# Routing the first expert phase in two halves, with larger DMA pieces and a reordered middle

## The reference

```
x = x + 0.5 * ffn(layernorm(x))
x = x + attn(layernorm(x))
x = x + 0.5 * ffn(layernorm(x))

ffn(x):  logits = x @ gate_w;  e = argmax(logits);  s = sigmoid(max(logits))
         shared = (silu(x @ sg) * (x @ su)) @ sd
         routed = (silu(s*x @ g[e]) * (s*x @ u[e])) @ d[e]
         return shared + routed
```

## Time and profile before

| | before |
|---|---|
| median of three runs | 646.51 us |
| the profiled execution, its own time | 639.84 us |
| its span | 638.1 us |
| TensorE busy | 545.6 us (86%) |
| VectorE busy | 453.0 us (71%) |
| ScalarE busy | 381.3 us (60%) |
| GpSimd busy | 147.9 us (23%) |
| moved by DMA | 40.69 MB, 52655 packets |

### The profile page before, as it was taken

How to read it: one execution, slowest core, us unless ns; L and a number is a source line. 1 busy time by engine, 2 the same in 40 slices (tenths; PEclk the granted TensorE clock), 3 DMA queues, 4 the chain that set the end, 5 groups by cost and what they waited for, 6 DMA issues and landing times.

```text
span 638.1 us, 13759 instructions
## 1 busy us (share of the span) xinstructions
PE 545.6 (86%) x4592; PEld 213.9 (34%) x4593; DVE 453.0 (71%) x832; ACT 381.3 (60%) x814; POOL 147.9 (23%) x236
## 2 busy tenths in 40 slices
PE   2983999935578999999999999999999977899991
PEld 2642344413221222222222222222224434534440
DVE  6561334436479899999999999999996567434442
ACT  2210344414322899999999999999997744134440
POOL 2563144534330000000000000000000034214552
PEclk9997899977655899999999999999999999889997
DMA  9997232221451000100001010000000001112114
GB/s 233 320 334 219 75 88 85 69 79 43 132 168 43 13 2 3 51 2 26 29 2 52 3 50 5 3 2 2 3 2 2 1 19 35 34 33 60 51 38 142
DMA packets 52655, 40.69 MB, mean 64 GB/s; under 512 B 5257, under 2 KB 49950, under 8 KB 52592
## 3 DMA queue, kind: packets, MB, share of 16 engines
q1 hardware_dynamic: 49520, 35.58, 19.2%
q0 software_dynamic: 3072, 4.28, 2.0%
HBM read 26.85 MB, written 14.88 MB: 65 GB/s over the span
## 4 chain that ended last, share of the span: by engine, by line
PE 71%; DVE 13%; DMA 6%; issue 4%; ACT 2%; POOL 2%; SPq 1%; POOLq 0%; ACTq 0%; DVEq 0%
PE bank L1399 22%; PE pair L1376 18%; PE pair L1264 8%; PE bank L1281 5%; DVE rowmax L1031 4%; PE pair L1273 3%; DMA xe<-rows 3%; PE pair L1124 2%; PE bank L1187 2%; POOL rows L514 2%; PE pair L1116 2%; ACT oT L747 1%; PE bank L1252 1%; PE bank L1388 1%; PE bank L1330 1%
## 5 line engine op out<-in xcount | busy, mean ns | idle before, releaser
L1031 DVE TENSOR_REDUCE rowmax<-pair 128x1 f32<-128x1024 f32 x256 | 294.6, 1217 | 15.6 <-PE pair L1376 15.5
L734 ACT ACTIVATE arena<-bank 128x512 f32<-128x512 f32 x500 | 271.1, 597 | 30.7 <-PE bank L1388 23.6
L1376 PE MATMUL pair<-k_stack,q_stack 48*128 48x512 bf16 x512 | 162.7, 403 | 11.0 <-DVE rowmax L1031 10.1
L1399 PE MATMUL bank<-arena 128*32 128x256 f32 x2048 | 161.3, 393 | 3.1 <-ACT oT L747 0.7
L1388 PE MATMUL bank<-q_stack,k_stack 51*128 51x512 bf16 x500 | 152.2, 387 | 0.4 <-ACT arena L734 0.4
L521 POOL DMA_INDIRECT y<-yb,slot_token x64 | 62.9, 982 | 97.9 <-ACT yb L647 94.0
L981 DVE TENSOR_TENSOR arena<-pair,arena 128x256 f32<-128x256 f32 x64 | 27.2, 425 | 78.9 <-ACT arena L642 70.6
L1399 PEld LDWEIGHTS bank<-arena 128*32 128x32 f32 x2048 | 43.4, 108 | 98.5 <-issue 63.5
L1264 PE MATMUL pair<-w_exp,xeT 128*64 x128 | 68.7, 619 | 0.4 <-ACT xeT L637 0.4
L1266 PE MATMUL pair<-w_exp,xeT 128*64 128x512 f32 x128 | 68.7, 619 | 0.0
L1376 PEld LDWEIGHTS pair<-k_stack,q_stack 48*128 48x128 bf16 x512 | 28.4, 95 | 117.8 <-DVE rowmax L1031 83.8
(11 more groups left out here) (187 smaller groups left out, 579.8 us busy)
## 6 DMA issues: line engine op xcount, KB each, us to landing
xe<-rows SPq DMA_DIRECT2D x64, 66.0 KB
w_exp<-in_r_gate SPq DMA_DIRECT2D x4, 1024.0 KB, 10.8
w_exp<-in_r_up SPq DMA_DIRECT2D x4, 1024.0 KB, 10.7
w_exp<-in_r_down SPq DMA_DIRECT2D x8, 512.0 KB, 10.6
rows<-empty_row SPq DMA_DIRECT2D x1, 2112.0 KB, 11.4
rows<-empty_row SPq DMA_DIRECT2D x32, 66.0 KB, 3.5
xnT<-y SPq DMA_DIRECT2D x8, 256.0 KB, 3.4
q_parts<-arena SPq DMA_DIRECT2D x12, 128.0 KB, 2.2
```

The lines of the kernel that those rows point to most:

```text
L734: nc.scalar.activation(prob[c % 2 * GH + head_of(u, c, k)], ring_bank("score", STEPS * u + i), ACT.Exp, scale=SCALE).then_inc(prob_ready, 1)
L1031: nc.vector.tensor_reduce(rowmax[u % 2][:, m:m + 1], pair[j % 2][:, :], AX_X, ALU.max).then_inc(smax_read, 1)
L1376: ins = nc.tensor.matmul(pair[j % 2][:, part * BANK:(part + 1) * BANK], q_stack[r][rows, half, l, t * P:(t + 1) * P], k_stack[r][rows, l, ...
L1399: ins = nc.tensor.matmul(bank[6][32 * h:32 * (h + 1), cols], v_grp[u % 2][:, c, h, :], prob[c % 2 * GH + h][:, cols], start=(c == 0 and w ...
```

## The change

- `TILES_OF` has four parts instead of three: the first phase's tiles 0 to 7 and 8 to 15, the second phase's 0 to 11 and 12 to 15. All uses of the part number follow (2 and 3 for the second phase).
- First phase: rows are normalised in two halves. `choose` is divided into `tops` (the maximum) and the rest. The first half is ranked and placed by its own counts, the second behind them (`ranks_behind(1)`, `more_pages(1)`, three more operations in `place_quad`). The logits of the second half go to another PSUM bank. The shared expert's products stand at other places between these steps, TensorE's `ranks(0)` ahead of `sh_up(0)`, `page_owners` behind `sh_up(5)`.
- Tokens lie otherwise in the tiles: partition p of a batch holds the tokens 8p to 8p+7, so that loads of x and of results and the store of the output move four tiles' rows of a partition in one piece (2 KB instead of 512 B). The token numbers that GpSimd writes into the rows follow.
- Blank rows are stored four at a time (2112 B instead of 528 B). The down matrices are loaded as pairs of rows (1 KB instead of 512 B), one DMA for eight experts instead of two; the expert product is written in the order that fits this.
- SyncE's first four page loads go ahead of the first four blank stores.
- GpSimd clears the attention's stacks behind the first phase's scatters.
- Middle: `store_norm(UNITS - 1)` goes behind the first placed quad instead of the third; in `ffn(1)` the fourth shared product and its Silu go ahead of the last quad's routing.

```diff
-TILES_OF = ((0, TILES), (0, FIRST_TILES), (FIRST_TILES, TILES))
+TILES_OF = ((0, TILES // 2), (TILES // 2, TILES), (0, FIRST_TILES), (FIRST_TILES, TILES))
...
+    def quad_rows(rows, g):
+
+        part = rows[g // 2 * BATCH_TILES * P:(g // 2 + 1) * BATCH_TILES * P, :].rearrange("(p t) h -> p t h", t=BATCH_TILES)
+        return part[:, 4 * (g % 2):4 * (g % 2) + 4, :]
...
+        blank_rows = q_stack[2][:, :, :, :].rearrange("p a l t -> p (a l t)").bitcast(F32)[:, 0:BLANKS * ROW]
...
-        ranks_bank = (bank[3], bank[0], bank[3])
-        ranks_at = [ranks_bank[k][:, 0:EXPERTS * (last - first)] for k, (first, last) in enumerate(TILES_OF)]
-        counts_at = (bank[4][:, 0:EXPERTS], bank[0][:, FIRST_TILES * EXPERTS:(FIRST_TILES + 1) * EXPERTS],
-                     bank[3][:, 4 * EXPERTS:5 * EXPERTS])
+        eid_row_at = (bank[3][0:1, 2 * P:3 * P], bank[3][0:1, 2 * P:3 * P])
+
+
+        ranks_area = (bank[3], bank[2], bank[0], bank[3])
+        logits_bank = (bank[2], bank[7], bank[2], bank[2])
+        ranks_at = [ranks_area[k][:, 0:EXPERTS * (last - first)] for k, (first, last) in enumerate(TILES_OF)]
+        counts_at = [bank[4][:, 0:EXPERTS]] + [ranks_area[k][:, EXPERTS * (last - first):EXPERTS * (last - first + 1)]
+                                              for k, (first, last) in enumerate(TILES_OF) if k]
...
-            sp.dma_start(rows_dram[0].rearrange("(j p) r -> p j r", p=P),
-                         empty_row[:, :].unsqueeze(1).broadcast_to([P, TURNS, ROW])).then_inc(prefilled[0], 16)
+            sp.dma_start(rows_dram[0].rearrange("(p j k) r -> p j (k r)", p=P, k=BLANKS),
+                         blank_rows.unsqueeze(1).broadcast_to([P, SLOTS // P // BLANKS, BLANKS * ROW])).then_inc(prefilled[0], 16)
...
-                for c in range(2):
-                    sp.dma_start(w3[:, e:e + step, 2 * INNER + c * P:2 * INNER + (c + 1) * P],
-                                 r_down[e:e + step, c * P:(c + 1) * P, :].rearrange("e p h -> p e h")).then_inc(experts_loaded, 16)
+
+                sp.dma_start(w3[:, e:e + step, 2 * INNER:],
+                             r_down[e:e + step].rearrange("e (p c) h -> p e (c h)", c=2)).then_inc(experts_loaded, 16)
...
-                    if n == 0:
-                        sp.dma_start(rows_dram[1][bass.ds(j * P, P), :], empty_row[:, :]).then_inc(prefilled[1], 16)
 
                 for r in range(4):
                     load(r, r)
+                if n == 0:
+                    for r in range(4):
+                        clear(r)
                 with sp.Fori(1, TURNS // 4) as k:
                     for r in range(4):
                         load(4 * k + r, r)
+                        if n == 0:
+                            clear(4 * k + r)
...
+            nc.gpsimd.memset(blanks[:, :, 0:P], 0.0)
+            nc.gpsimd.memset(blanks[:, :, P:ROW].bitcast(I32), NOWHERE).then_inc(consts_ready, 1)
             nc.gpsimd.memset(empty_row[:, 0:P], 0.0)
-            nc.gpsimd.memset(empty_row[:, P:ROW].bitcast(I32), NOWHERE).then_inc(consts_ready, 1)
+            nc.gpsimd.memset(empty_row[:, P:ROW].bitcast(I32), NOWHERE)
...
+                    clear_stacks()
...
-            clear_stacks()
...
-                    transposed(0)
+                    transposed(0, 0, 2)
+                    transposed(0, 2, 4)
                     score_exp(0)
+                    score_exp(1)
                 else:
                     for i in range(3):
                         sh_silu(i)
                     transposed(2, QUADS - 1)
-                    score_exp(2)
-                for i in range(3 * n, 2 * QUADS):
+                    sh_silu(3)
+                    score_exp(3)
+                for i in range(4 * n, 2 * QUADS):
...
+            def tops(k):
+
+                tiles = slice(*TILES_OF[k])
+                if k == 2:
+                    dve.wait_ge(pv_done, CHUNKS * (UNITS - 2))
+                dve.wait_ge(logits_ready, k + 1)
+                nc.vector.tensor_reduce(top[:, tiles], by_tile(logits_bank[k])[:, tiles], AX_X, ALU.max).then_inc(top_ready, 1)
...
+            def used_pages():
+
+                nc.vector.tensor_scalar(full_to[:, :], count_i[:, :], float(PAGE), None, ALU.add)
+                nc.vector.tensor_copy(more_i[:, 0:1], spare_to[:, EXPERTS:EXPERTS + 1])
+                after(nc.vector.tensor_tensor(spare_2[:, :], spare_at[:, :], count_i[:, :], ALU.subtract))
+                after(nc.vector.tensor_tensor(spare_2[:, :], spare_2[:, :], base_e[:, :], ALU.subtract))
...
-                if k == 2:
+                if k % 2:
...
-                    normalize(0)
+                    normalize(0, 0, 2)
+                    normalize(0, 2, 4)
+                    tops(0)
                     choose(0)
                     chances(0)
+                    weigh_rows(0)
+                    tops(1)
+                    spare_pages(0)
+                    place_quad(0, 0)
+                    place_quad(0, 1)
                     sh_product(0, 0)
-                    weigh_rows(0)
-                    spare_pages(0)
-                    for g in range(QUADS):
-                        place_quad(0, g)
-                        if g < 3:
-                            sh_product(0, g + 1)
+                    used_pages()
+                    choose(1)
+                    chances(1)
+                    weigh_rows(1)
+                    sh_product(0, 1)
+                    more_pages(1)
+                    place_quad(1, 2)
+                    sh_product(0, 2)
+                    place_quad(1, 3)
+                    sh_product(0, 3)
...
-                    choose(2)
-                    chances(2)
-                    weigh_rows(2)
-                    more_pages()
-                    place_quad(2, last)
                     sh_product(1, 3)
+                    tops(3)
+                    choose(3)
+                    chances(3)
+                    weigh_rows(3)
+                    more_pages(3)
+                    place_quad(3, last)
...
-                    nc.vector.tensor_tensor(h_sb[r % 2], bank[r % 2][:, INNER:2 * INNER], silu_sb[r % 2][:, 0:INNER],
-                                            ALU.mult).then_inc(h_done, 1)
+
+                    by_pair = lambda a: a.rearrange("p (i c) -> p i c", c=2)
+                    nc.vector.tensor_tensor(h_sb[r % 2].rearrange("p (c i) -> p i c", c=2), by_pair(bank[r % 2][:, INNER:2 * INNER]),
+                                            by_pair(silu_sb[r % 2][:, 0:INNER]), ALU.mult).then_inc(h_done, 1)
...
-                choose(1)
-                chances(1)
-                weigh_rows(1)
-                spare_pages(1)
-
-                for g in range(QUADS - 1):
-                    place_quad(1, g)
-                nc.vector.tensor_scalar(full_to[:, :], count_i[:, :], float(PAGE), None, ALU.add)
-                nc.vector.tensor_copy(more_i[:, 0:1], spare_to[:, EXPERTS:EXPERTS + 1])
-                after(nc.vector.tensor_tensor(spare_2[:, :], spare_at[:, :], count_i[:, :], ALU.subtract))
-                after(nc.vector.tensor_tensor(spare_2[:, :], spare_2[:, :], base_e[:, :], ALU.subtract))
+                tops(2)
+                choose(2)
+                chances(2)
+                weigh_rows(2)
+                spare_pages(2)
+
+                place_quad(2, 0)
                 store_norm(UNITS - 1)
+                place_quad(2, 1)
+                place_quad(2, 2)
+                used_pages()
...
-            def ranks_behind():
-
-                pe.wait_ge(slots_ready, 2 * QUADS - 1)
-                for t in range(FIRST_TILES):
-                    hot = onehot[1][:, t * EXPERTS:(t + 1) * EXPERTS].unsqueeze(1).broadcast_to([P, 5, EXPERTS])
-                    nc.tensor.matmul(bank[3][:, 0:5 * EXPERTS].rearrange("p (b e) -> p b e", e=EXPERTS), onesb[:, :], hot,
+            def ranks_behind(k):
+
+                first, last = TILES_OF[k]
+                blocks = last - first + 1
+                if k == 3:
+                    pe.wait_ge(slots_ready, 2 * QUADS - 1)
+                for t in range(first):
+                    hot = onehot[k // 2][:, t * EXPERTS:(t + 1) * EXPERTS].unsqueeze(1).broadcast_to([P, blocks, EXPERTS])
+                    nc.tensor.matmul(ranks_area[k][:, 0:blocks * EXPERTS].rearrange("p (b e) -> p b e", e=EXPERTS), onesb[:, :], hot,
                                      start=(t == 0), stop=False)
...
+                    ranks(0)
                     sh_up(0)
-                    ranks(0)
+                    ranks_behind(1)
                     sh_up(1)
+                    ranks(1)
                     sh_up(2)
                     sh_up(3)
                     sh_down(0)
-                    page_owners()
                     sh_up(4)
                     sh_up(5)
+                    page_owners()
```

(37 more changed lines are left out.)

58 lines of the change are left out of this document (29 added, 29 removed).

## The result

The changed kernel took 638.01 us in the median (637.26 to 638.81, 4 runs) against 646.20 us of the kernel before on the same chip: a ratio of 0.9875, 95% interval 0.985 to 0.9899. Two later sets on other occasions gave 0.9929 (0.9903 to 0.9954; 639.27 us, before 644.13 in 27 runs) and 0.9914 (0.9881 to 0.9947; 640.26 us, before 644.92). By the medians it is 4.7 to 8.2 us faster. The time lies inside the range on record, but the gain is well short of the 13.0 us that the sum promised: the profiled execution took 637.26 us (span 635.5), where the sum gave 626.8.

What follows compares the result with a forecast made beforehand. GpSimd's scatter queue was taken to set the first expert phase, with DMA full beside it. Gains of 5.8 (first phase), 0.3 (before attention), 6.0 (middle) and 0.9 (ends) made 13.0, from 646.51 to 633.5 us; range 627 to 641.

Steps and rivals of the forecast that it cites:

- Routing of the first phase: First expert phase, in two halves: first scatter at 28.4 (5.4 us earlier), ninth at 39.3, sixteenth at 48.3 (4.8 earlier).
- The rival of a late second half: First routing: second half comes four us late, 9.0 us gained in all, 637.5 us; chance 0.16.
- The stream's end, 51.5: First phase: with larger pieces the weight stream ends at about 51.5 instead of 57.3, hidden.
- First phase, 5.8: Routing and page loads of the first phase: second page lands at 59.05 instead of 64.85, 5.8 us gained.
- 58.2 here at most: 0.9 of slack: First phase: the shared expert's tail, 15.7 us after 42.5, ends by 58.2, leaving 0.9 us of slack.
- Middle, 6.0: End of attention to second expert phase: the reorder gains 6.0 us, bounds 3.35 and 7.
- From there to the maximum (536.46) the order is kept: Middle, VectorE from residual to maximum: same order, so the residual's 3.5 us gain carries through, about 3.35 earlier.
- Ends: Results' return and output store in 2 KB pieces: 0.9 us gained; with the 0.3 before attention, bounds 0 and 2.
- Larger pieces in the stream: First-phase weight stream: 367 GB/s for 293 (down weights, 2.9 us) and 257 (blank rows, 3.0 us), hidden.
- no penalty shows: Expert product written with a stride of 128: no penalty expected from 0.425 us; up to some 1.65 us is free.
- the likeliest case's own range: Whole kernel, likeliest case: 633.5 us with its own range 630 to 637.5; chance 0.62.
- a late second half together with a small middle: Whole kernel, both shortfalls at once (first routing late, middle giving only 3.35): would still save 6.5 us.

Runs made afterwards that it cites:

- before, again: Kernel before, unchanged, profiled a second time: 643.98 us in the median, profiled span 643.7.
- pieces: Kernel before with only the larger DMA pieces, their token order and the strided product: 0.9972 of before, 1.8 us.
- middle: Kernel before with only the reordered middle and the fourth shared product's move: 0.998 of before, 1.3 us.
- middle, stop: Kernel before with the reordered middle, GpSimd stopping before the second routing's ninth scatter until the last quad's logits are written: 638.96 us, 0.9901 of before.
- halves: Changed kernel with pieces, token order and middle taken back, leaving the split first routing, page-load order and later stack clearing: 0.9953 of before, 3.0 us.
- after, again: Changed kernel, unchanged, profiled a second time: first page at 58.11 us.
- after, third: Changed kernel, unchanged, profiled a third time: first page at 64.25 us.
- after, stop: Changed kernel, GpSimd stopping before the second routing's ninth scatter until the last quad's logits are written: 633.35 us, 0.9811 of before.
- after, pace 1.8: Changed kernel with the shorter GpSimd memset before each of scatters two to twelve of the second routing: 633.93 us, 0.9807 of before.
- after, pace 2.2: Changed kernel with the longer GpSimd memset before each of scatters two to twelve of the second routing: 635.29 us, seen once.
- after, stop and void wait: Changed kernel with the second-routing stop, plus a first-routing wait for the first shared-expert down-projection that did not pause GpSimd: 632.22 us, 0.9804 of before.
- after, two stops: Changed kernel with the second-routing stop, plus one before the first routing's ninth scatter until the fifth shared-expert piece is written: 630.61 us, 0.9766 of before.

## Why the prediction was right, and where it was wrong

Every profile cut at the same marks (us; "tail" is the end of the last shared-expert addition of the first phase; the third and fourth lengths count from the second phase's first row scatter):

| profile | tail | first page | first scatter to last maximum | to first page | turns | last store to end |
|---|---|---|---|---|---|---|
| before | 54.0 | 63.0 | 16.5 | 39.2 | 68.4 | 10.4 |
| before, again | 63.0 | 64.0 | 18.9 | 40.0 | 71.8 | 10.7 |
| pieces | 63.1 | 64.1 | 18.9 | 40.0 | 70.2 | 10.1 |
| middle | 62.0 | 63.1 | 19.6 | 39.6 | 69.0 | 10.6 |
| middle, stop | 63.9 | 64.8 | 13.4 | 35.2 | 70.6 | 10.4 |
| halves | 60.0 | 61.0 | 19.0 | 40.1 | 72.4 | 10.8 |
| after | 61.8 | 62.8 | 19.8 | 39.7 | 68.6 | 10.0 |
| after, again | 57.0 | 58.1 | 19.6 | 39.6 | 70.0 | 10.0 |
| after, third | 63.3 | 64.3 | 19.8 | 39.8 | 70.2 | 9.8 |
| after, stop | 63.9 | 64.8 | 13.3 | 35.2 | 69.7 | 9.9 |
| after, pace 1.8 | 60.6 | 61.8 | 12.7 | 34.2 | 69.7 | 9.6 |
| after, pace 2.2 | 58.1 | 59.1 | 12.6 | 36.2 | 72.2 | 10.0 |
| after, stop and void wait | 58.1 | 59.1 | 13.3 | 33.5 | 70.0 | 9.6 |
| after, two stops | 56.7 | 58.6 | 13.3 | 35.2 | 69.4 | 10.0 |

*Routing of the first phase: right.* First scatter 28.4 forecast, 28.19 measured; ninth 39.3 and 38.70; sixteenth 48.3 and 47.63. The rival of a late second half is out. The stream's end, 51.5, was right too.

*First phase, 5.8: mis-sized by a bound that fell.* The step "58.2 here at most: 0.9 of slack" for the shared expert was taken from a stretch of an execution without holds. In the changed kernel the tail ended at 61.8, 57.0 and 63.3, because signals were held. The first page came at 61.7 in the mean of three, 2.3 us before that of the repeated kernel before. The mechanism holds: where the tail is free (two stops), the page sets the start at 58.57, even with the last scatter 2.7 us later.

*Middle, 6.0: the step that failed.* "From there to the maximum (536.46) the order is kept" left out a wait that no row showed. The residual addition came earlier as forecast (5.35 us after the attention's last transposes for 9.05, that is 3.7 for 3.5), the maximum did not: the copy waits until about 2 us after the twelfth scatter, in either order. To the first page 0.3 is left (40.0 to 39.7). With the run broken most of the forecast returns: the maximum 3.1 to 3.8 us sooner than in the one profile of before without a hold (12.6 to 13.4 for 16.5; forecast 3.35), the first page 3.1 to 5.7 (forecast 6.0).

*Ends: right, 0.9 forecast, 0.7 measured* (10.6 us in the mean of five profiles with small pieces, 9.9 of nine with large ones). *Larger pieces in the stream: right in rate, hidden in time, as costed;* all pieces together gave 1.8. The 0.3 for two quads ahead of the attention was not measured by itself. The Trainium skill's 512 B for line rate ("DMA: Bandwidth & Descriptors", Specifications) does not fit this stream: 257 GB/s with rows of 528 B, 345 with four of them in one. *Stride: "no penalty shows" was wrong by 0.19 us a product,* within the 1.65 us that the prediction had found free.

*The base.* The prediction left the 6.7 us between the profile of before and its runs "as it is". It was a warning that the profile was of an unusual execution: all other timings of before, 641.9 to 648.6, lie above its 639.84. Cut at the marks, the repeated before is 5.5 us longer: 1.0 to the first page, 0.8 in the middle, and 3.3 in the second phase's turns. These turns vary from 68.4 to 72.4 over all profiles with no order that follows an edit, and stay unexplained. So the total came out in the range by luck: a sum twice too large was set off from the longer median, and 638.01 even lies above the likeliest case's own range, 630 to 637.5, so that only the widening by 3 us holds it. Set off from the profiled execution, the same sum gave 626.8. With both runs of scatters broken the changed kernel is 14.3 us below before by the medians; how much of that is the forecast 13.0 and how much a hold that the kernel before has too, no run separates.

One small sum is off: a late second half together with a small middle leaves 0.8 + 1.0 + 0.3 + 3.35 + 0.9 = 6.35, and not 6.5. Nothing else hangs on it.

## What to carry to other kernels

An engine that only feeds a queue can delay others by the rate at which it feeds: here thinning GpSimd's scatters, which lengthens its own work, gained 1.5% where bringing TensorE's work forward in the middle had gained 0.2%. When an end stands microseconds before the wait that it should release, compare the recorded increments across two or three executions before moving work. And a profile that lies outside its own timed runs may not be like them: take another before a slack of 0.9 us is built on it.

## What the runs showed of the hardware

- Row scatters of 128 rows of 528 B every 1.27 us let TensorE's signals through for the first six to nine of an unbroken run and held them from the eighth to eleventh on, for up to 12.0 us. Most come in bunches, the last 1.3 to 2.8 us after the run's last scatter. After the stop of 3.1 us the next run held one from its fifth scatter on, for 1.0 us. At 1.8 and 2.2 us a scatter there was no hold in twelve scatters. VectorE's and ScalarE's signals passed.
- One of fourteen profiles (the first of before) had no hold. In the others 19 to 26% of the increments of the ten semaphores between TensorE, VectorE and ScalarE in the expert turns are missing from the record, in that one 4%, and in the attention none anywhere. So the hold may be tied to the recording itself. The timed runs fit with it, as their medians fell when it was broken; but each of them has a span and a clock on record too, so none is known to have run without recording, and the cause of the hold stays open.
- A row scatter that began 0.06 us after the start of a VectorE product of 128x1024 took 2.00 us in five profiles; those that began at or ahead of its start took 0.95 to 0.96.
- After 5.95 us of standing still in a hold TensorE came back at half clock (granted 0.50 at 534 to 537): the logits of 535.07 took 1.91 us. In the paced kernel (granted 1.00) they took 1.04.
- A VectorE product of 128x256 took 425 ns written contiguously, 618 ns with single floats 512 bytes apart.
